# A transformer stage on one Trainium2 core: attention scores in 64x32 array tiles, and new orders of work

## The reference

```python
q, k = l2norm(q) * qs, l2norm(k) * ksc          # 16 heads of 64, then rotary factors
sim = jnp.einsum('bhwie,bhwje->bhwij', bq, bk2) * QK_SCALE   # windows of 32 queries, 64 keys
attn = jax.nn.softmax(jnp.where(mask, -big, sim), -1)
x = einsum('bhwij,bhwje->bhwie', attn, bv2) @ Wo + x
x = (a * gelu(gate)) @ W2 + b2 + x              # a, gate = layernorm(x) @ W1 + b1
```

## Time and profile before

| | |
|---|---|
| median of 3 runs | 2218.1 us (2202.98 to 2225.02) |
| the profiled execution | 2217.59 us, span of the core 2215.7 us |
| mean granted TensorE clock over the span | 0.938 |
| busy, share of the span: PE, PEld, DVE, ACT, POOL | 90%, 61%, 78%, 75%, 57% |
| layers, first projection to last transpose | 440 to 2010 us |

### The profile page before, as it was taken

How to read it: one execution, slowest core, us unless ns; L and a number is a source line. 1 busy time by engine, 2 the same in 40 slices (tenths; PEclk the granted TensorE clock), 3 DMA queues, 4 the chain that set the end, 5 groups by cost and what they waited for, 6 DMA issues and landing times. The chain is left out here.

```text
span 2215.7 us, 55457 instructions
## 1 busy us (share of the span) xinstructions
PE 1990.7 (90%) x20349; PEld 1357.6 (61%) x20349; DVE 1739.2 (78%) x3618; ACT 1660.6 (75%) x3144; POOL 1265.8 (57%) x1132
## 2 busy tenths in 40 slices
PE   5799898679999999999999999999999999984283
PEld 2333333246777777777777777777777777773252
DVE  4666654488999999999999999999999999935523
ACT  2255656368999999999999998999999999964123
POOL 4500000277777777777777777777777777722053
PEclk8699989789999999999999999999999999997587
DMA  6412100201111111111211113111311111100512
GB/s 157 110 43 45 24 3 2 69 27 40 30 40 31 40 60 54 36 40 30 80 40 35 36 30 90 30 40 30 89 30 40 30 40 30 39 22 26 194 36 69
DMA packets 70562, 107.36 MB, mean 48 GB/s; under 512 B 20887, under 2 KB 47774, under 8 KB 68734
## 3 DMA queue, kind: packets, MB, share of 16 engines
q1 hardware_dynamic: 68262, 100.87, 15.8%
q0 software_dynamic: 1280, 2.62, 0.4%
q10 hardware_dynamic: 752, 0.33, 0.1%
HBM read 41.60 MB, written 12.26 MB: 24 GB/s over the span
## 5 line engine op out<-in xcount | busy, mean ns | idle before, releaser
L1583 POOL TENSOR_TENSOR qk<-rot_cos,rot_sin 128x512 f32<-128x512 f32 x256 | 323.5, 1274 | 79.3 <-DVE rot_sin L1361 79.3
L1593 POOL TENSOR_TENSOR qk<-qk,rnorm 128x512 f32<-128x512 f32 x256 | 263.2, 1044 | 117.4 <-DVE rnorm L1394 117.4
L1359 DVE TENSOR_TENSOR rot_cos<-pA,layer_tab 128x512 f32<-128x512 f32 x384 | 262.4, 683 | 58.5 <-ACT sq L1171 54.3
L434 ACT ACTIVATE probs_by_key<-pT 128x512 f32<-128x512 f32 (+3 forms) x384 | 177.3, 489 | 163.3 <-PE pT L320 127.4
L499 DVE TENSOR_REDUCE minus_max<-pS 128x1 f32<-128x1024 f32 (+7 forms) x256 | 184.5, 753 | 116.7 <-PE pS L290 116.0
L1371 DVE TENSOR_REDUCE sumsq<-sq 128x8 f32<-128x512 f32 x384 | 251.1, 665 | 19.7 <-ACT sq L1171 19.6
L1171 ACT ACTIVATE sq<-pA 128x512 f32<-128x512 f32 x384 | 228.5, 595 | 50.2 <-PE pA L890 40.7
L1361 DVE TENSOR_TENSOR rot_sin<-pA,layer_tab 128x512 f32<-128x512 f32 x384 | 260.7, 679 | 0.0
L1231 ACT ACTIVATE probsT<-pD 64x512 f32<-64x512 f32 x380 | 224.0, 589 | 34.3 <-PE pD L931 30.9
L1600 POOL TENSOR_TENSOR probs<-probs,row_inverse 128x1024 f32<-128x1024 f32 x96 | 182.5, 1902 | 97.4 <-DVE row_inverse L1430 97.4
L1191 ACT ACTIVATE qT<-pC 64x512 f32<-64x512 f32 x384 | 226.0, 588 | 7.3 <-PE pC L905 0.5
(11 more groups left out here) (342 smaller groups left out, 4577.5 us busy)
## 6 DMA issues: line engine op xcount, KB each, us to landing
v_shifted<-v SPq DMA_DIRECT2D x96, 384.0 KB, 3.5
v_shifted<-v SPq DMA_DIRECT2D x95, 128.0 KB, 3.4
q_stack<-stacked SPq DMA_DIRECT2D x24, 192.0 KB
k_stack<-stacked SPq DMA_DIRECT2D x24, 192.0 KB
W_ahead<-in_Wqkv_dram SPq DMA_DIRECT2D x12, 384.0 KB
layer_weights<-in_Wqkv_dram SPq DMA_DIRECT2D x12, 384.0 KB
stacked<-part SPq DMA_DIRECT2D x32, 128.0 KB, 2.4
tokens_in<-tokens SPq DMA_DIRECT2D x2, 1024.0 KB
```

Source lines behind the costliest of these rows:

```text
L1359: dve.tensor_tensor(t1[c % 2][:, :].rearrange("p (h g d) -> p h g d", g=2, d=32), a, tabl[s % 2][:, j].unsqueeze(1).broadcast_to([P, 8, 2, ...
L1583: pool.tensor_tensor(qk(s, c), t1[c % 2][:, :], t2[c % 2][:, :], ALU.add).then_inc(added[c], 1)
L1593: pool.tensor_tensor(v, v, rn[p % 2][:, o:o + 8].unsqueeze(2).broadcast_to([P, 8, DH]), ALU.mult).then_inc(scaled[c], 1)
```

## The change

The scores take one step for both banks: `S(p, k)` in place of `S(0, p, k)` and `S(1, p, k)`. A matmul contracts the 64 rows of one head with 32 query columns, with no zeros beside them, in a 64x32 tile of the array; eight of them in a row go to eight different positions (`b` picks the row half and the bank, `j` and `z` the column position). There are 64 matmuls a tile where there were 32, for the same products. `qT` shrinks to [P, 8, P] and its zeroing goes; `qt` becomes one copy of 128 partitions. Heads come to lie in another order over banks and partitions, which `PV` undoes by its indices. `s_ready` becomes one semaphore; `PV` waits for both `pt_kept`; `pev` and `vev` wait for both `o_ready`; `qt` and `kt` wait for the one `s_ready`. The five bank functions go. The round now starts at the half with the output projection, a half round earlier than before, so that there are 49 bodies in place of 50 and a longer `drain()`, which is the ordinary order with the missing steps left out. The orders of all four engines are new in detail. `FILL` is 0 and `spare` is called nowhere, so they emit nothing.

```diff
-            def S(u, p, k):
+            def S(p, k):
                 s = tile(p, k)
-                pe.wait_ge(q_kept[u], s + 1)
-                pe.wait_ge(masked[u], s + 1)
-                for hp in range(4):
-                    for wi in range(4):
-                        j, wp = wi % 2, wi // 2
-                        o = s % 2 * P + 32 * wi
-                        mm = pe.matmul(C[u][64 * j:64 * j + 64, hp * P + 64 * wp:hp * P + 64 * wp + 64],
-                                       qT[:, 4 * u + hp, wi, :, :], KT[:, 4 * u + hp, o:o + 64],
-                                       start=False, stop=True, skip_group_check=True)
-                mm.then_inc(s_ready[u], 1)
+                for u in range(2):
+                    pe.wait_ge(q_kept[u], s + 1)
+                    pe.wait_ge(masked[u], s + 1)
+                for a in range(4):
+                    for wp in range(2):
+                        for z in range(2):
+                            for j in range(2):
+                                for b in range(2):
+                                    hp, row = 2 * a + z, slice(64 * b, 64 * b + 64)
+                                    q, o = 64 * wp + 32 * j, k * P + 64 * wp + 32 * j
+                                    mm = pe.matmul(C[b][64 * j + 32 * z:64 * j + 32 * z + 32, a * P + 64 * wp:a * P + 64 * wp + 64],
+                                                   qT[row, hp, q:q + 32], KT[row, hp, o:o + 64],
+                                                   start=False, stop=True, skip_group_check=True)
+                mm.then_inc(s_ready, 1)
...
             def PV(u, p, k):
-                pe.wait_ge(pt_kept[u], s + 1)
+                for b in range(2):
+                    pe.wait_ge(pt_kept[b], s + 1)
...
             def qt(u, p, k):
-                for b in range(2):
-                    rows = slice(64 * b, 64 * b + 64)
-                    a = act.activation(qT[rows, 4 * u:4 * u + 4, :, b, :],
-                                       C[u][rows, :].rearrange("p (h w q) -> p h w q", h=4, w=4), AF.Copy)
-                a.then_inc(q_kept[u], 1)
+                act.activation(qT[:, 4 * u:4 * u + 4, :], C[u][:, :].rearrange("p (h q) -> p h q", h=4), AF.Copy).then_inc(q_kept[u], 1)
```

More of the change, by code:

```diff
@@ L361, in _ @@
                 job(j)
+            for _ in range(FILL):
+                pe.wait_ge(ident_cast, 1)
+                pe.wait_ge(mask_in, 16)
             for it in range(GROUPS + 2):
@@ L988, in Wa, with spare @@
                     return
-                hidden(p, W1_AT, a_ready, middle_banks(p))
+                hidden(p, W1_AT, a_ready, F)
+            def spare(n):
+                for _ in range(n):
+                    pe.wait_ge(x_turned, 4)
             def turn_out(n, bank):
@@ L1151, in _ @@
                 mm.then_inc(x_turned, 1)
-            for r in range(PAIRS + 2):
+            for r in range(PAIRS + 1):
                 if r == 0:
@@ L1177, in vev @@
                 act.wait_ge(v_ready[v], s + 1)
-                ge(act, o_ready[v], s - 2)
+                for u in range(2):
+                    ge(act, o_ready[u], s - 2)
                 if s > 1:
@@ L1227, in pev @@
                 act.wait_ge(pt_ready[u], s + 1)
-                ge(act, o_ready[u], s)
+                for b in range(2):
+                    ge(act, o_ready[b], s)
                 for wp in range(2):
@@ new lines, in drain @@
+                oev(0, LAST - 2, 1)
+                vev(0, LAST, 0)
+                ex(0, LAST - 1, 1)
+                vev(1, LAST, 0)
+                oev(1, LAST - 2, 1)
+                qt(1, LAST, 1)
+                qt(0, LAST, 1)
+                ge_(LAST - 3)
+                pev(1, LAST - 1, 0)
+                kt(1, LAST, 1)
+                kt(0, LAST, 1)
+                mk(1, LAST, 1)
+                mk(0, LAST, 1)
+                pev(0, LAST - 1, 0)
+                ex(1, LAST, 0)
@@ new lines, in drain @@
+                oev(1, LAST - 1, 0)
+                vev(0, LAST, 1)
+                oev(0, LAST - 1, 0)
+                ex(0, LAST, 0)
+                vev(1, LAST, 1)
+                ex(1, LAST, 1)
+                pev(0, LAST - 1, 1)
+                xnT(LAST - 2)
+                pev(1, LAST - 1, 1)
+                oev(0, LAST - 1, 1)
+                ex(0, LAST, 1)
+                oev(1, LAST - 1, 1)
+                ge_(LAST - 2)
+                pev(1, LAST, 0)
+                pev(0, LAST, 0)
@@ L1647, in _ @@
             pool.wait_ge(env["aside_stored"], 64)
-            pool.wait_ge(zeroed, 7)
+            pool.wait_ge(zeroed, 6)
             pool_body(pool, -1)
-            for r in range(PAIRS + 2):
+            for r in range(PAIRS + 1):
                 pool_body(pool, r)
```

611 lines of the change are left out of this document (367 added, 244 removed).

## The result

| | before | after |
|---|---|---|
| median of 4 runs each | 2211.4 us | 2250.2 us |
| ratio, 95% interval | | 1.019 (1.014 to 1.023) |
| profiled execution, span of the core | 2217.59, 2215.7 us | 2251.26, 2249.4 us |
| first `W2` to the 43rd (42 rounds) | 1338.3 us | 1375.7 us |

The change made the kernel 1.9% slower, where 2174 us was forecast. Of the 34 us between the two spans, the 42 full rounds hold 37.4; the drain behind them got about 3 us longer, and the stretch ahead of the first `W2` about 3 shorter (567.56 before, 564.12 after). So the loss lies in the rounds.

The account below looks back on a forecast made before the run. PE was taken to bound the round of 31.85 us, with DVE next at 29.41. From 2217.6 us, 44 rounds at 1.05 took off 46 and the drain added 3, giving 2174; the range was 2135 to 2235.

Parts of the forecast that it names:

- rival 3: PE's instruction queue: code packets of 256 instructions arrive late at the scores, 0.6 us for each of 88, 2227 us; chance 0.05.
- the sum for a round: Whole round: PE's floor 30.15 us, DVE's work 29.41, bounds 30.15 and 31.85; taken as 30.8, 1.05 gained.
- Price of a pass: Scores on PE: a 64x32 pass costs 8 ns, 256 passes make 2.05 us, so PE gains 1.7 a round.
- changes of tile shape: PE between scores, values and 128x128 work: six a round before and after, the same 1.0 us in sum.
- The two fifths: Whole round: placed two fifths of the way from 31.85 to 30.15 us, at 30.8.
- rival 2: DVE becomes the bound; ping-pong over two projection banks holds the round at about 31.4 us, 2201 us in all; chance 0.08.
- ACT's saving: Query copies: four of eight 588 ns copies a round go, 2.35 us of ACT; direct worth zero, cover for PE's order.
- rival 5: Scores stand ahead of both PV and wait for both masks; at 1.5 us a tile, +1.3 a round, 2278 us; chance 0.09.
- the 0.78 of cover: Half with the output projection, before: time from the second mask copy's end at 1037.87 to the scores' start at 1038.65.
- (1): Scores on PE: the two 64-row halves share a column tile's feed, 14.6 ns a pass, no gain, 2221 us; chance 0.07.
- (4): Scores on PE: matmul pace has a floor near 29.2 ns; at 25 ns +2.66 us a round, 2338 us; chance 0.09.
- The drain: Last three pairs: Wa waits for the gelu, 1.2 us, faster scores give some back; bounds 0 and 8, taken as +3 us.

Follow-up runs that it names:

- e1_aligned: The changed kernel with ten more waits in TensorE's queue each round and 34 ahead of the layers, 1024 TensorE instructions a round: 2171.9 us, ratio 0.983 to the kernel before.
- e5_two_copies: e1_aligned with the copy of the transposed queries made in two copies of 64 partitions in place of one of 128: 2286.7 us, ratio 1.036 to the kernel before.
- e6_positions: e1_aligned with four orders of a tile's 64 score matmuls, one for each tile number modulo 4, same products: 2263 us, one run.
- the borders a little further: e1_aligned with FILL 8 in place of 34, block borders 201 and 179 instructions behind the scores' start: 2245.3 us, ratio 1.018 to the kernel before.

## Why the prediction was wrong

**Where it failed.** The forecast of 2174 is what the kernel does without the holes: e1_aligned measured 2171.9. The whole of the miss is rival 3, code loading, which the sum for a round holds at nothing. Its chance was put at 0.05, and its price at 0.6 us for each of 88 scores, 53 us; the 42 rounds show 89 (1.06 for each of 84, weight loads and clock included). The step that failed is the sentence that set the evidence against it: that today's stream of scores and values, at 14.6 ns an instruction, had only one wait in 1300 us. That was read as "a dense stream does no harm". It was a statement on one pace alone: 256 x 14.6 = 3.74 us a block (3.87 for the shortest in the trace), and the next block arrives 2.3 to 3.9 us behind the border. The old block lay at the upper end of that, and the change cuts it to 1.4 to 2.8 us. All that was needed stood in the prediction: 256 instructions a packet, 1.1 us a packet as a lower bound, and 256 instructions in 1.0 us afterwards. The fetch time between 1.1 and 3.74 was open, and with about half of that range or more above the new block the chance had to be near even.

**The cost per hole** was too small too. From the border to the next block it is 2.3 to 3.9 us, not the 1.1 of the packet: the packet itself mostly starts 0.5 to 1.5 us behind the border, and PE goes on 2.2 to 2.8 us after it starts. And a hole at a weight load costs more than itself. DMA share and clock in the changed kernel's stretches around the hole of 4.59 us (columns as above):

```profile
1612.00:1619.60 7.60, 7.60 (x189) 5.58 (x188) 7.43 (x13) 5.95 (x12) 7.42 (x7) 1.00 0.75 247
1624.40:1626.40 2.00, 1.97 (x27) 1.85 (x28) 0.00 (x0) 0.04 (x1) 0.00 (x0) 0.50 0.29 33
1626.40:1628.40 2.00, 2.00 (x3) 0.89 (x4) 0.00 (x0) 1.25 (x3) 0.00 (x0) 0.50 0.03 0
1628.40:1630.40 2.00, 2.00 (x6) 0.94 (x5) 0.00 (x0) 1.38 (x3) 0.00 (x0) 0.50 0.19 53
1630.40:1632.40 2.00, 2.00 (x10) 1.53 (x9) 1.83 (x4) 0.14 (x1) 0.46 (x1) 0.93 0.75 213
```

With the DMA engines at 0.75 the block took 6.9 us (border at 1617.5, PE on at 1624.43), and behind the hole the granted clock is 0.50, the 1.2 GHz level, for some 6 us: a projection takes 1.70 us there (1627.99 to 1629.69) where it takes 0.86 in the earlier trace rows, so about half of the 6 us is lost, 3.0 as an estimate. With a second hole of 0.9 us this is the round of 39.32: 4.8 + 3.0 + 0.9 = 8.7 over 30.63.

**Price of a pass.** Taken as 8 ns; measured 11.0 with the entry (1.41 / 128), 9.98 within the run. PE's gain was forecast as 1.7 a round and is 31.85 - 30.64 = 1.21. The three groups of scores of that round took 1.08 + 1.04 + 1.87 = 3.99 to the next step's start (two stand in the earlier trace rows, the third ran from 1022.61 to 1023.65) and take 2 x 1.41 = 2.82, which is 1.17 of it. That leaves 0.04 for the changes of tile shape outside these groups, which I had taken to stay as they were.

**The two fifths.** Forecast 30.8, measured 30.63: of the 1.7 I gave 1.05 to the round, and all of the real 1.21 arrived. Two errors, a pass too cheap and orders too pessimistic, cancelled; that 30.8 came so close is luck. DVE at 29.27 of 30.64 did not hold PE (rival 2).

**ACT's saving was mis-valued.** The text had four copies fewer, "its direct worth is zero", and cover for the order. The 2.45 us a round of e5_two_copies says it is the condition of the new orders: without it PE waits for the mask and for the query copy, as rival 5 described, at 2287 us. The prediction named the 0.78 of cover, the 0.2 it would be short, and the saving that gives it back. The sign of that balance was right, its size was not: without the saving PE is short of 1.2 us at the mask and of 0.8 at the keys, and the word zero hid that.

**Rivals.** (1) Row halves in turns, 14.6 ns a pass: e6_positions excludes it with 9.98 for eight positions, and with the same 23.5 for two row halves as for two columns. (2) DVE: above. (4) A floor near 25 to 29 ns: 9.98 ns a pass held over 128 passes excludes it. The Trainium skill's rule in "TensorE: Matmul & The Clock Gate", section "Wait — 56ns, not 53.3ns?", of about 25 ns from start to start at least, is contradicted by these runs in 64x32 tiles: by 9.98 ns with eight positions in turns and 13.15 with four. (5) The order: not in this kernel, for the reason above.

**The rest.** The drain was put at +3 and is +3: from the 43rd `W2` to the last transpose, 2046.37 - 1939.80 = 106.6 where it was 2009.49 - 1905.83 = 103.7. Of its parts, the wait of `Wa` for the gelu is there as said (it answers to the earlier trace rows):

```profile
2036.17 2.93 PE L973 MATMUL pE<-xnT,layer_weights 128*128 128x256 f32 x6 [1.28 <-ACT ff_gateT L1339]
```

The sign that I had set for rival 3, single holes of 0.5 to 1 us that wander from round to round, is what the trace shows (most of them lie in the values behind the scores), with holes of up to 2 us, and of about 4.7 at three weight loads.

## What to carry to other kernels

Count instructions as well as time. Before a run of matmuls is cut into more and smaller ones, compare how long 256 instructions last with how long a block takes to arrive: here 2.3 to 3.9 us, near 7 beside heavy DMA traffic. A kernel just above that bound shows no sign of it, and a longer block is no guarantee (the borders a little further). If the loop is long and regular, make its instruction count a multiple of the block and choose the place of the border: with ten fillers in the loop, 34, 8 or 176 in front gave 2172, 2245 and 2310 us. Take the place from a trace in which it drifts, not from block lengths. And when a change saves work on an engine that bounds nothing, ask what the new order spends it on.

## What the runs showed of the hardware

- TensorE's code comes in packets of 256 instructions (3.47 MB in 212 packets for 54,321). Behind a dense block PE went on 2.3 to 3.9 us after the border and 2.2 to 2.8 us after the packet's start; behind sparse work the packet started 2 to 7 us after the border.
- 64x32 tiles in eight positions in turns take a pass of 64 columns every 9.98 ns, weight load included, four column positions 13.15, two positions 23.5; row and column positions count alike.
- A hole of 4.6 us in TensorE's work was followed by some 6 us at 0.50 of the clock. Behind the hole of 1.30 us four passes of the values kept their 0.12 us and the granted clock stayed at 1.00 (1606.10 to 1608.00), so that one cost no clock.
